# Results of the second expert layer scattered to token order from inside the loops and read back contiguously, with its rows routed in four parts

## The reference

```python
flat = rms_norm(x, norm_scale)            # each token scaled
scores = flat @ w_router.T                # 8 experts
two best experts and their weights for each token
h = moe_linear(flat, expert, w_up)        # 128 -> 512, row i takes its own expert's matrix
h = h[:, :256] * silu(h[:, 256:])         # gate
y = moe_linear(h, expert, w_down)         # 256 -> 128
out[token] += weight[token, c] * y[token, c]     # c = 0, 1: the two choices
```

## Time and profile before

| | |
|---|---|
| median of 3 runs | 1219.71 us (1217.18 to 1224.35) |
| span of the profiled execution | 1213.9 us, first to last instruction; its time with what lies around the span is not among the figures, the median lies 5.8 us above the span |
| instructions | 24398 |
| linear stage | about 783 to 1008 us |
| loop 2, loop 3, tail | 1008 to 1093, 1099 to 1164, 1164 to 1214 us |
| busy in the span | PE 83%, ACT 65%, DVE 52%, POOL 36% |

### The profile page before, as it was taken

How to read it: one execution, slowest core, us unless ns; L and a number is a source line. 1 busy time by engine, 2 the same in 40 slices (tenths; PEclk the granted TensorE clock), 3 DMA queues, 4 the chain that set the end, 5 groups by cost and what they waited for, 6 DMA issues and landing times.

```text
span 1213.9 us, 24398 instructions
## 1 busy us (share of the span) xinstructions
PE 1005.2 (83%) x9150; PEld 536.7 (44%) x9150; DVE 629.7 (52%) x1874; ACT 786.7 (65%) x1178; POOL 435.5 (36%) x425
## 2 busy tenths in 40 slices
PE   4679898999999999999888988787988877897930
PEld 3432222222222322222177877544544446786930
DVE  5556758443644334303155546678777644644722
ACT  1558798889999999999833745655544423464510
POOL 4121212131102222635011555545532671365545
PEclk9889999999999999999998989899988987998965
DMA  5360811800168103001011333100000111233522
GB/s 159 76 95 18 131 23 36 131 6 1 36 96 197 31 1 118 25 29 33 13 39 53 112 99 96 52 18 19 19 12 1 34 44 29 85 110 110 144 70 67
DMA packets 85355, 74.97 MB, mean 62 GB/s; under 512 B 11960, under 2 KB 79416, under 8 KB 84344
## 3 DMA queue, kind: packets, MB, share of 16 engines
q1 hardware_dynamic: 75444, 55.61, 20.2%
q0 software_dynamic: 8192, 16.79, 4.9%
q10 hardware_dynamic: 1604, 0.99, 0.3%
HBM read 39.28 MB, written 33.95 MB: 60 GB/s over the span
## 4 chain that ended last, share of the span: by engine, by line
PE 46%; DVE 19%; ACT 18%; issue 6%; POOL 5%; DMA 3%; another core or an unknown queue 1%; DVEq 1%; SPq 1%; ACTq 0%; POOLq 0%
ACT attn_probs L1382 16%; PE ps L1839 9%; PE ps L1087 8%; PE ps L830 5%; PE ps L1070 5%; PE ps L1853 4%; POOL moe_back L1779 3%; PE ps L650 3%; DVE lin_scores L2287 2%; PE ps L2159 2%; PE ps L1824 2%; PE ps L2083 1%; PE ps L2173 1%; PE ps L1561 1%
## 5 line engine op out<-in xcount | busy, mean ns | idle before, releaser
L1382 ACT ACTIVATE attn_probs<-ps 128x1024 f32<-128x1024 f32 x512 | 481.1, 1083 | 55.6 <-PE ps L1070 55.1
L1087 PE MATMUL ps<-attn_probs,attn_v 128*18 128x512 f32 x2048 | 272.6, 604 | 4.9 <-DVE room L1333 4.0
L1768 POOL DMA_INDIRECT slots<-moe_xr,moe_slot x128 | 125.5, 980 | 153.9 <-issue 77.2
L1070 PE MATMUL ps<-stack 50*128 50x512 bf16 x1024 | 167.8, 386 | 12.1 <-DMA stack<-qk_parts 2.2
L1779 POOL DMA_INDIRECT moe_back<-results,moe_slot x128 | 124.3, 971 | 94.6 <-PE ps L1824 31.3
L1070 PEld LDWEIGHTS ps<-stack 50*128 50x128 bf16 x1024 | 36.1, 94 | 252.3 <-ACT attn_probs L1382 235.7
L1839 PE MATMUL ps<-lin_scores 128*128 128x128 f32 x960 | 130.5, 290 | 0.0
L1839 PEld LDWEIGHTS ps<-lin_scores 128*128 128x128 f32 x960 | 123.7, 206 | 1.6 <-DVE lin_scores L1897 0.8
L1962 ACT ACTIVATE lin_scores<-ps 128x256 f32<-128x256 f32 x156 | 56.9, 381 | 99.5 <-PE ps L1839 88.1
L1853 PE MATMUL ps<-stack,lin_scores 128*128 x624 | 85.7, 281 | 3.7 <-DVE lin_scores L1904 3.1
L1853 PEld LDWEIGHTS ps<-stack,lin_scores 128*128 128x128 f32 x624 | 77.8, 195 | 6.0 <-issue 6.0
(11 more groups left out here) (237 smaller groups left out, 1494.1 us busy)
## 6 DMA issues: line engine op xcount, KB each, us to landing
moe_gathered<-slots SPq DMA_DIRECT2D x76, 128.0 KB
results<-lin_heads_out SPq DMA_DIRECT2D x76, 128.0 KB
stack<-qk_parts SPq DMA_DIRECT2D x36, 256.0 KB, 9.0
qk_parts<-moe_xr SPq DMA_DIRECT2D x32, 128.0 KB, 2.4
qk_parts<-moe_xr SPq DMA_DIRECT2D x16, 192.0 KB, 11.2
stack<-in_expert_w SPq DMA_DIRECT2D x1, 3072.0 KB
slots<-zeros SPq DMA_DIRECT2D x1, 3008.0 KB, 12.8
slots<-zeros SPq DMA_DIRECT2D x1, 2496.0 KB, 21.7
```

The source lines that it names most:

```text
L1070: instruction = T.matmul(k.ps[:, SCORE_BANKS[i % 3][s], :], d.stack[b % 2][rows, 1, pair, kt * P:(kt + 1) * P], d.stack[b % 2][rows, 0, pa ...
L1087: instruction = T.matmul(k.ps[32 * j:32 * j + STRIP, PV_BANK, :], d.v[:, b % 2, kt, first:first + STRIP], d.probs[:, n % A_PROBS, j * BANK ...
L1382: A.activation(d.probs[:, n % A_PROBS, 2 * e * BANK:2 * (e + 1) * BANK], k.ps[:, banks[0]:banks[1] + 1, :].rearrange("p a n -> p (a n)"), ...
L1768: G.indirect_dma_start(out=k.dram["slots"][half][0:SLOT_TILES[r] * P], out_offset=bass.IndirectOffsetOnAxis(ap=d.slot[:, FIRST[r] + at, c: ...
```

## The change

It concerns rounds 2 and 3 only (`SENT = 2`); rounds 0 and 1 keep gathers and stores.

- Routing is in six rounds of routing, `R_SIZE = (20, 12, 8, 8, 8, 8)`: two of eight token tiles for each of the loops 2 and 3. Routing rounds 2, 3 and 4 have their chains in the linear stage, routing round 5 in loop 2.
- Rows are scattered to `sent_slots`, which has a fixed region of 17 tiles for each expert, so that the places of the first part don't depend on the second part's counts. Each row has 129 columns: the last holds the row's place in token order (token x 2 + choice). POOL scatters the first choices of eight tiles, waits until they have landed (`second`), adds 1 to the column, and scatters the second choices.
- `roff` becomes `dve_sent_table` (17 DVE operations for 3), once for each loop: it finds for each slot tile the row in `sent_slots` at which it begins. SP writes eight blank tiles behind the experts' last rows (`sp_blank_rows`), then loads tile by tile at a row that it reads into a register, 39 loads for 20.
- In the loop DVE works out the target rows (`moe.dest`) of each unit from column 129, ACT writes the result to a ring of 16 units, and POOL scatters it straight to token order in `sent_results` (`pool_send`). SP's stores are gone.
- SP reads the results back contiguously, four token tiles in a DMA (`read`, 512 KB), four reads for each loop; the 64 gathers of rounds 2 and 3 are gone. The adds and the output DMAs stay.

```diff
+R_SIZE, R_FIRST, ROUND_OF = (20, 12, 8, 8, 8, 8), (0, 20, 0, 8, 16, 24), (0, 1, 2, 2, 3, 3)
+SENT = 2
+NY, SENT_GROUP = 16, 4
+READ_AT, MERGE_AT = (12, 13, 22, 26), (18, 22, 28, 32)
+def row_transfers(q):
+    first, second = ([("scat", q, at, c) for at in range(R_SIZE[q])] for c in range(TOPK))
+    return first + [("second", q)] + second
...
-        if ("lstats", 1) in out:
-            routes += [None] * ROUTE_WAIT + spread(route_part(2, 0, 2))
-        if ("lstats", 3) in out:
-            routes += close_route(2, 2, 4)
-        if ("lstats", 5) in out:
-            routes += [None] * ROUTE_WAIT + loose_route(3, 0, 2)
-        if ("rplace", 2) in extra:
-            scatters = transfers("scat", 2)
+        for q in range(SENT, len(R_SIZE) - 1):
+            if ("lstats", 2 * (q - SENT) + 1) in out:
+                routes += [None] * (ROUTE_WAIT if q == SENT else 0) + close_route(q, 0, 2)
+            if ("rplace", q) in extra:
+                scatters = scatters + row_transfers(q)
...
     elif r == 2:
-        works = [list(route_part(3, 2, 4)) + list(route_slots(3))]
+        works = [list(route_part(5, 0, 2)) + list(route_slots(5))]
+    elif r == 3:
+        for g in range(SIZES[2] // TPG):
+            slots[READ_AT[g]].append(("read", 2, g))
...
+        elif kind == "second":
+            G.wait_ge(k.e_rows[ROUND_OF[r] - SENT], rows_through(r) - 16 * R_SIZE[r])
+            own = d.xr[:, R_FIRST[r]:R_FIRST[r] + R_SIZE[r], DIM]
+            G.tensor_scalar(own, own, 1.0, None, ALU.add).then_inc(k.e_second, 1)
+            G.wait_ge(k.e_second, r - SENT + 1)
...
+        elif kind == "read":
+            g = piece[2]
+            if g == 0:
+                for j in range(NY // SENT_GROUP):
+                    S.wait_ge(k.e_sent[r - SENT][j], sent_through(r, j, UNITS[r]))
...
+            rows = k.dram["sent_results"][r - SENT][0:SIZES[r] * P * TOPK].rearrange("(n p c) d -> p n c d", p=P, c=TOPK)
+            S.dma_start(read_area(k, r, g), rows[:, g * TPG:(g + 1) * TPG, :, :]).then_inc(read_done(k, r, g)[0], 16)
...
+        if r >= SENT:
+            tiles = slice(u * UNIT, u * UNIT + width)
+            V.tensor_tensor(k.moe.dest[:, r - SENT, tiles], k.moe.gathered[:, u % NG, 0:width, DIM], k.moe.spare[:, tiles],
+                            ALU.min).then_inc(k.e_dest, 1)
...
+def pool_send(G, k, r, u):
+    bank, n = k.use["edown", r, u]
+    G.wait_ge(k.free[bank], n + 1)
...
+    for i in range(unit_width(r, u)):
+        j = u * UNIT + i
+        G.indirect_dma_start(out=k.dram["sent_results"][r - SENT],
+                             out_offset=bass.IndirectOffsetOnAxis(ap=k.moe.dest[:, r - SENT, j:j + 1], axis=0),
+                             in_=k.loop.y_sent[:, at % NY, i, :], in_offset=None
+                             ).then_inc(k.e_sent[r - SENT][at // SENT_GROUP % (NY // SENT_GROUP)], 16)
...
+        for i in range(unit_width(r, u) if r >= SENT else 0):
+            j = u * UNIT + i
+            row = S.value_load(k.moe.rows[0:1, r - SENT, j:j + 1], min_val=0, max_val=EXPERTS * REGION - P)
+            S.dma_start(k.moe.gathered[:, u % NG, i, 0:ROW],
+                        k.dram["sent_slots"][r - SENT][bass.ds(row, P), :]).then_inc(k.e_gather[u % NG], 16)
```

More of the change, by code:

```diff
@@ L497, in plan_linear @@
     assert not any(routes)
-    k.l_left = [piece for work in works for _, piece in work] + scatters
+    k.l_left = [piece for work in works for _, piece in work]
+    k.scatters_left = scatters
     fill(k.l_left)
@@ L544, in plan_loop @@
                 out.append(k.l_more.pop(0)[1])
-    assert not works and (r != 2 or ("rweight", 3) in [piece for one in slots for piece in one])
+    assert not works and (r != 2 or ("rweight", 5) in [piece for one in slots for piece in one])
     plan = [(slots[2 * u], slots[2 * u + 1]) for u in range(UNITS[r] + 3)]
@@ L1877, in loads_through, with gathered_through, rows_through, sent_unit @@
     return UNITS_BEFORE[r] // NG + u // NG + 1
+def gathered_through(r, u):
+    units = [(q, v) for q in range(r + 1) for v in range(u % NG, UNITS[q] if q < r else u + 1, NG)]
+    return sum(unit_width(q, v) if q >= SENT else 1 for q, v in units)
+def rows_through(q):
+    return 16 * TOPK * sum(size for p, size in enumerate(R_SIZE[:q + 1]) if ROUND_OF[p] == ROUND_OF[q])
+def sent_unit(r, u):
+    return UNITS_BEFORE[r] - UNITS_BEFORE[SENT] + u
+def sent_through(r, j, end):
+    groups = NY // SENT_GROUP
+    return 16 * sum(unit_width(r, u) for u in range(end) if sent_unit(r, u) // SENT_GROUP % groups == j)
 def scattered_through(half):
@@ L2045, in sp_loop, with sp_blank_rows @@
             side(piece)
+def sp_blank_rows(S, k, r):
+    S.wait_ge(k.e_offsets, r + 1)
+    if r == SENT:
+        S.wait_ge(k.fill_laid, 1)
+    for e in range(EXPERTS):
+        row = S.value_load(k.moe.stop_i[0:1, r - SENT, e:e + 1], min_val=0, max_val=EXPERTS * REGION - P)
+        S.dma_start(k.dram["sent_slots"][r - SENT][bass.ds(row, P), :], k.fill[:, :]).then_inc(k.e_blanked, 16)
+    S.wait_ge(k.e_blanked, 16 * EXPERTS * (r - SENT + 1))
 def inter_before(u):
@@ L2267, in dve_masks @@
     V.tensor_scalar(d.later[:, :, :], causal, -1.0, 1.0, ALU.mult, ALU.add)
+    moe, slot_tile = k.moe, k.const["slot_tile"]
+    for r in range(SENT, ROUNDS):
+        V.tensor_scalar(moe.xr[:, FIRST[r]:FIRST[r] + SIZES[r], DIM], slot_tile[:, 0:SIZES[r]], float(TOPK * P), None, ALU.mult)
+    V.tensor_scalar(moe.spare[:, :], slot_tile[:, 0:max(SLOT_TILES[SENT:])], float(P), float(TOPK * P * max(SIZES[SENT:])),
+                    ALU.mult, ALU.add)
+    V.memset(k.fill[:, 0:DIM], 0.0)
+    V.memset(k.fill[:, DIM:ROW], NOWHERE).then_inc(k.fill_laid, 1)
 def dve_linear(V, k):
@@ L2647, in macaron_kernel @@
         last = ROUNDS - 1
-        k.e_last = transfers("gath", last)
+        k.e_last = [("read", last, g) for g in range(SIZES[last] // TPG)]
         for at in range(SIZES[last]):
```

226 lines of the change are left out of this document (157 added, 69 removed).

## The result

| | kernel before | changed kernel |
|---|---|---|
| median of the runs | 1218.74 us (1217.18 to 1224.35) | **1241.24 us** (1234.25 to 1245.62) |
| profiled execution, its span | 1213.9 us | 1234.25 us, span 1232.4 us |

The ratio is 1.0156, with a 95% interval of 1.0101 to 1.021: slower by over 0.5%, and 20 us above the upper end of the range given.

What follows compares the result with a forecast made beforehand. It took PE to bound loop 3 and POOL's indirect DMAs the tail. Its span, 1213.9 - 22 - 4 + 12 + 1 = 1200.9 us, plus 5.8 to the median, gave 1206.7, say 1206 us; range 1193 to 1221.

Steps and rivals of the forecast that it cites:

- The tail: After the last result: sends, landing, four reads, adds and last output take 28.5 us for 50.3, a gain of 22 us.
- Rival 5: Tail: the reads are slow, at 66 GB/s, so the gain is 6 us and the time 1223; chance 0.05.
- The boundary: Between loops 2 and 3: the last scatter is issued earlier, a gain of 4 us of PE's 6.4 us wait.
- The linear stage: Three routing chains for one put 14.7 us more on DVE: a loss of 12 us, between 3 and 22.
- Rivals 1 and 2: Linear stage: first, chains hide, loss 3, time 1198, chance 0.2; second, chains cost double, loss 22, 1217, chance 0.12.
- SP's loads: Loops 2 and 3: two register loads and two DMAs cost SP 2.2 us a unit, hidden under PE's 3.03.
- Rival 4: Loops 2 and 3: SP becomes the bound, with register loads at 1.3 us adding 22 us: 1229; chance 0.10.
- Inside the loops: Loops 2 and 3: PE's and ACT's work unchanged, POOL's sends 2.5 us a unit against PE's 3.03; loss of 1 us.
- the four small things: Loops 2 and 3: shorter chain with longer table, one DVE operation a unit, POOL's sends, blank tiles; together 1 us lost.
- rival 3: Loop 2: POOL falls behind at 1.4 us an indirect DMA, boundary gain gone, sends end 5 us later: 1216; chance 0.13.
- Its own sign of being wrong: Loop 3 should keep 3.0 to 3.1 us a unit; the forecast is wrong if that unit time moves.
- the forecast of the difference: Whole kernel: the span changes by -13 us, the sum of the predicted terms.

Runs made afterwards that it cites:

- e15: The changed kernel, unedited, run again on a chip without late signals: 1184.81 us, 0.9878 times the kernel before.
- e4: The kernel before, with loop 2's 32 row scatters of round 3 no longer waiting for TensorE's products: 1199.74 us, ratio 1.0000.
- e8: The changed kernel with rounds 2 and 3 routed in one chain of 16 tiles each: 1216.21 us, 1.0138 times the kernel before.
- e2: The changed kernel with SP's loads of loops 2 and 3 from constant rows, without register loads: 1186.61 us, 0.9881 times the kernel before.
- e3: The changed kernel with loop 2's row scatters waiting again for TensorE's products: 1188.67 us, 0.9886 times the kernel before.
- e11: The changed kernel with loop 2's scatters waiting for TensorE's products and loop 3's loads from constant rows, chip with late signals: 1241.15 us, ratio 1.0114.
- e12: The changed kernel with constant rows in both loops and SP storing loop 3's results without POOL's sends, chip with late signals: 1224.35 us, ratio 0.9987.
- e14: The changed kernel with loop 2's scatters put behind its sends, chip without late signals: 1234.26 us, ratio 1.0271; loop 2 83.4 us.
- e5: The changed kernel, unedited, run again on a chip without late signals: 1187.03 us, 0.9901 times the kernel before.
- e7: The changed kernel, unedited, run a third time, without a late signal: 1186.76 us, 0.9899 times the kernel before.

## Why the prediction was wrong, point by point

**The tail: right, a little short.** The gain was 26.7 us where 22 was forecast. By its own steps:

```profile
1208.54 0.28 ACT L2085 ACTIVATE lin_q_masked<-ps 128x128 f32<-128x128 f32 x1 [0.56 <-PE ps L1936]
...
1215.28 0.92 SPq L1876 DMA_DIRECT2D moe_back<-sent_results  x2
...
1219.20 0.35 DVE L1730 SCALAR_TENSOR_TENSOR x<-moe_back,moe_weight,x 128x128 f32<-128x128 f32 x1 [11.65 <-DMA moe_back<-sent_results]
...
1229.71 0.37 SPq L1867 DMA_DIRECT2D out<-x  x1
```

From the last result to the first read 6.5 us (forecast 6.35); the first read 3.9 (4); the adds 10.5 (12.3); the last output 2.7 (5.8). The first is right by luck: the last send was issued 5.1 us behind the last result (forecast 3.6) and SP read 1.3 us later (2.75); in e15 it was 3.7 and 1.3. The last two were mis-sized. The output DMA itself did not change: its last packet ends 1.9 us behind its issue in either trace. What went was an end that I had counted with it. In the kernel before SP then stands at the end of the program (L2653), until POOL gets there 3.1 us later than SP; in the changed kernel POOL is there at the same time. What POOL does between its last gather and that point the trace doesn't show. The line of before:

```profile
SPq L2653 <- PEq L2653: 3.3, 1, 3.3
```

Rival 5 is out.

**The boundary: right.** PE waits 0.8 us where it waited 6.4, better than the forecast 2.4. On the first chip the long loop 2 helped: the last scatter was issued 26 us ahead of PE's last product. The step itself is confirmed by e15, where the last scatter comes 79.3 us behind the first turn (forecast 79.0) and 7.5 us ahead of PE's last product, and PE waits 1.1.

**The linear stage: right on the first chip.** 238 us against 225, DVE busy 168.8 where it was 155.1, so 13.6 more of the 14.7 reckoned. On the other chips the changed kernel's first turn lay at 1009.3 to 1015.0 and e4's at 1000.7, +9 to +14. e8 confirms the cause: with the routing of before in the stage, 7.5 us come back. Rivals 1 and 2 are out.

**SP's loads: right.** The engine's own records of loop 3 show a register load, a bounds check and the DMA in 1.10 us a tile, 2.2 us a unit as reckoned; e2 without register loads gained nothing that can be measured against e3 (0.9881 and 0.9886, intervals overlapping), and e11 and e12 show the long loops without them. Rival 4, whose 1229 us comes nearest to the measured time, had the wrong cause. The register load by itself is 0.27 us in most of SP's 78. The Trainium skill's floor of about 600 ns for it (DMA: Bandwidth & Descriptors, section Latency and other measured facts) does not fit, and the measurement decides: ACT's loads are 0.28 us as well, the one in the earlier trace rows too, where the prediction had read 0.62 us, an upper bound, as agreement. The Trainium skill's figure of about 1.3 us for loads from HBM (Runtime: NRT & Kernel Launch, section The ~15µs preamble/postamble breakdown) is nowhere near them.

**Inside the loops: this is the step that failed.** "I count a loss of 1 us for the four small things" stands against 27.8 us in loop 2 and 10.5 in loop 3. It priced the sends by POOL's own time, 2.5 us a unit under PE's 3.03, and asked only whether POOL keeps up. POOL did keep up: an issue still took 0.97 us and rival 3's 1.4 us never came. Its own sign of being wrong came, too: loop 3's units grew by 0.5 us each. What the runs showed in its place is a price that POOL's work puts on TensorE's signals on some chips: POOL issues 60 row transfers in loop 2 where it issued 31, and what had been 18 us of lateness became 121. Without such signals the term is still too small: loop 2 is longer by 7.4 and loop 3 by 1.3, against a variant of the kernel before. Of the 7.4, e14 gives back 3.4 by taking the scatters out from between the sends; the table's 17 operations in one block stand for more of it, by the trace alone (PE's turn waits 4.5 us for DVE behind it in e15, and 3.3 on the first chip); this was not tried apart.

**Could it have been seen?** Its sign could, its size could not: no row of before leads from 18 us of lateness to 121. The chain of before has 1% for an unknown queue, and among its waits of ACT in loop 3 stands

```profile
ACT lin_heads_out L1968 <- remote: 4.2, 4, 1.2
```

I read the rows of that trace as what a unit costs, and they already held what POOL's 32 transfers a loop cost there. On the chips without it the forecast of the difference, -13 us, is what was measured: -13.0 in the spans of e4 and e15, and -12.9 to -17.6 between the medians of e5, e7 and e15 and the kernel before beside them. There the terms differ from mine by up to 7 us and cancel, so that the agreement of the sum is in good part luck.

**What stays open.** Which part of the chip holds the signals up, and whether the chip makes the difference or what runs beside the kernel. Every time here is of an execution of which at least the span was recorded; whether the recording has a share in the delay wasn't tried. Why the same lateness costs more in the new loop 3 (46 us of it, 74.6 us where a chip without has 63.2) than in the old (39 to 44 us of it, 64.1 to 64.6 us where a chip without has 61.9); gathers and sends go opposite ways, which no run set against each other. And whether sends that leave POOL idle half the time would win on both sorts of chip: no kernel tried beats the changed one where signals are on time, and none of those that compute the whole result beats the kernel before where they are late.

## What to carry to other kernels

Count an engine's DMA issues as a load on the others' signals, and not only as time of its own queue: before moving row transfers into a loop, compare stretches of the trace with and without them, in how soon after a product its reader starts. Waits for "remote" or "issue" while no engine is full (PE at 75% here) are the sign to look at. And run the unchanged kernel again beside the first cure: here two edits "cured" a loop that was short on that chip without them.

## What was unexpected of the hardware

- On the chips with late signals, TensorE's semaphore signals came up to 10.3 us after the end of its product while POOL issued indirect DMAs back to back (0.97 us each, 0.30 between), and within 2.4 us once it paused. On four chips none was over 0.3 us late with the same instructions.
- In such stretches TensorE and SP themselves crept: three times in loop 2 products of L1922 came 0.7 us apart where 0.11 is the rule, and some of SP's instructions that take 0.01 to 0.03 us took 0.6 to 0.7. In e15's loop 2 neither happens.
- Plain DMA traffic at 124 GB/s, with SP issuing it, made no signal late (e12, loop 3).
- The granted clock in the second part of loop 2 was 0.84 with the stalls and 0.96 without: a part of the loss is products at the lower of the two levels behind stalls, where those of L1922 come 0.21 us apart and not 0.11 (66 times in loop 2, 38 in e15).
